# Second slice finished in sorted order, with rows that carry x1, gate, probability and place, and the first slice's rows modulated by GpSimd

## What is computed

```
mod = (silu(c) @ wmod) -> sa, ca, ga, sb, cb, gb            # per sequence, 128 each; ga, gb clamped away from 0
h  = layernorm(x) * (1 + ca) + sa
q, k = silu(h Wq), silu(h Wk);  k normalised;  v = h Wv;  beta = 2 sigmoid(h Wbet);  a = sigmoid(h Wf)
for t: Sd = a_t S;  S = Sd + beta_t k_t (v_t - k_t Sd);  o_t = q_t S
x1 = x + ga * ((rmsnorm(o) * norm_w) @ Wo)
h  = layernorm(x1) * (1 + cb) + sb
route = softmax(h @ router_w + router_b);  e = argmax, p = max
out = x1 + gb * p * (silu(h W1a[e]) * (h W1b[e])) @ W2[e]
```

## Time and profile before

| | us |
|---|---|
| median of 3 runs | 469.03 (467.74 to 471.08) |
| profiled execution, its time | 469.78 |
| profiled execution, its span | 468.0 |
| busy: DVE / PE / ACT / POOL | 377.9 / 368.5 / 281.0 / 276.6 |
| recurrence ends (last products on DVE) | 303.2 |
| last `sum_outputs` ends | 307.0 |
| last expert matmul ends | 453.2 |

### The profile page before, as it was taken

The page is one execution under the profiler, slowest core; times in us unless marked ns, Lnnn a source line. Parts: engine busy times, 40 slices in busy tenths (PEclk is TensorE's granted clock), DMA queues, the critical chain, the costliest instruction groups (busy, mean ns, idle before and its releaser), DMA issues.

```text
span 468.0 us, 8624 instructions
## 1 busy us (share of the span) xinstructions
PE 368.5 (79%) x2495; PEld 317.9 (68%) x2495; DVE 377.9 (81%) x1143; ACT 281.0 (60%) x634; POOL 276.6 (59%) x339
## 2 busy tenths in 40 slices
PE   3867853938779996993867866879989999999970
PEld 2322410728567766993967866879888999999970
DVE  4859999999998999999997999976828445569634
ACT  3589766956357466586646626374774657566520
POOL 1036234999999949757678198704185556653340
PEclk9989987878879999898698796999999999999995
DMA  8184888992000002923200004117411114155006
GB/s 229 39 118 94 109 114 119 137 127 3 0 1 1 1 1 90 373 78 66 71 0 1 1 7 117 60 41 162 150 30 41 41 41 115 46 164 139 28 34 179
DMA packets 49502, 37.13 MB, mean 79 GB/s; under 512 B 11088, under 2 KB 45200, under 8 KB 49328
## 3 DMA queue, kind: packets, MB, share of 16 engines
q1 hardware_dynamic: 46064, 30.39, 32.9%
q0 software_dynamic: 3392, 6.18, 4.3%
HBM read 17.36 MB, written 10.29 MB: 59 GB/s over the span
## 4 chain that ended last, share of the span: by engine, by line
PE 32%; DVE 30%; POOL 13%; issue 11%; ACT 7%; DMA 6%; SPq 1%; ACTq 0%; POOLq 0%; DVEq 0%
PE bank L900 9%; PE bank L636 6%; DVE U L1797 6%; DVE S L1810 5%; DVE p L1791 5%; DVE p L1804 4%; PE bank L917 4%; PE bank L693 3%; POOL sorted_h L1085 3%; POOL big L1019 2%; DMA sorted_h<-X,pos 2%; POOL prod_o L308 2%; ACT ph L1197 2%; PE bank L638 1%; PE bank L697 1%
## 5 line engine op out<-in xcount | busy, mean ns | idle before, releaser
L693 PE MATMUL bank<-prod_o,ID 128*128 128x128 f32 x512 | 75.5, 308 | 30.3 <-POOL prod_o L315 18.4
L900 PE MATMUL bank<-Q,p 128*128 128x128 f32 x736 | 94.2, 275 | 1.2 <-ACT p L1507 1.2
L693 PEld LDWEIGHTS bank<-prod_o,ID 128*128 128x128 f32 x512 | 70.5, 219 | 33.1 <-POOL prod_o L315 21.7
L900 PEld LDWEIGHTS bank<-Q,p 128*128 128x128 f32 x736 | 89.0, 192 | 1.5 <-ACT p L1507 1.4
L1312 ACT ACTIVATE p<-S,GAM 128x64 f32<-128x64 f32 x126 | 48.4, 410 | 66.9 <-DVE S L1810 66.2
L308 POOL TENSOR_TENSOR prod_o<-Q,ST 128x1024 f32<-128x1024 f32 x28 | 60.0, 2143 | 29.4 <-PE bank L697 29.2
L1143 POOL DMA_INDIRECT placed_y<-Q,place x46 | 44.4, 965 | 49.4 <-DVE place L2003 17.9
L1507 ACT ACTIVATE p<-big 128x1024 f32 x46 | 48.5, 1057 | 40.9 <-PE bank L900 38.9
L1810 DVE TENSOR_REDUCE S<-p 128x64 f32<-128x320 f32 x126 | 55.8, 475 | 0.0
L1797 DVE TENSOR_REDUCE U<-p 128x32 f32<-128x288 f32 x128 | 52.2, 442 | 0.0
L1791 DVE TENSOR_TENSOR p<-S,bank 128x256 f32<-128x256 f32 x128 | 48.7, 410 | 0.7 <-ACT bank L1307 0.7
(11 more groups left out here) (265 smaller groups left out, 746.1 us busy)
## 6 DMA issues: line engine op xcount, KB each, us to landing
big<-in_L_ffn_w_dram SPq DMA_DIRECT2D x1, 4096.0 KB, 14.1
big<-big SPq DMA_DIRECT2D x16, 192.0 KB, 4.5
Q<-sorted_h SPq DMA_DIRECT2D x46, 64.5 KB, 2.2
sorted_h<-ZERO SPq DMA_DIRECT2D x2, 1472.0 KB, 17.8
X<-in_L_attn_x_dram SPq DMA_DIRECT2D x8, 256.0 KB, 4.6
big<-big SPq DMA_DIRECT2D x16, 128.0 KB, 5.4
K<-placed_y SPq DMA_DIRECT2D x8, 256.0 KB, 3.2
out_dram<-X SPq DMA_DIRECT2D x8, 256.0 KB, 2.4
```

Of the source, the lines that this page charges most:

```text
L693: pe.matmul(ps, ID[:, :], prod_o[:, k % 2, i, :], start=(i == 0), stop=False, skip_group_check=True)
L900: m = pe.matmul(bank[(1, 6)[g % 2] + k][:, c * P:(c + 1) * P], W1E[g % 2][:, f:f + P], XST[:, g % 3, :], start=True, stop=True)
```

## The change

Second slice. The rows scattered to `sorted_h[1]` are 386 floats wide instead of 129: the modulated row, x1, the gate row gb, the place and the probability. x1 is written by `attend` on DVE straight into the wide rows (X1), the gates are loaded into them (GB, now two transfers, issued when the variances of slice 1 are there), and the probability too, so `exponentials(1)` moves on ACT from g = 22 to g = 10 and `probability(1)` on DVE to just ahead of `sort(1)`. `ys` for g >= 23 is two DVE instructions: result * probability * gate, then + x1; POOL scatters this straight to `out`, with a bounds check that drops the padding rows. `load_y`, `finish` and `store_out` of slice 1 are gone, and so are the sixteen L2091. The padding on SP grows from four to seven transfers. A ring slot of slice 1 is free only when `ys` has used the row.

First slice. PE turns the normalised tiles, ACT copies them unmodulated (`copy_turned_first`, four of 128x512), the router's weights carry the scale and ones times the shift (`modulate_router`, moved on POOL from behind the loop to g = 7). `shift2`, `shift_rows`, `turn_back` and `rows` are gone. POOL modulates the rows behind `make_products(11, 1)`, eight instructions, with scales and shifts that SP spreads earlier. `logits(0)` and `sort(0)` come one chunk earlier on DVE. On POOL the first burst of six scatters lies behind `make_products(12, 1)`, the second of five between (13, 0) and (13, 1), the third of five behind (13, 1); before, six lay between (13, 0) and (13, 1) and ten behind.

```diff
-    AT_SHIFT = (AT_ROWS + 2, AT_ROWS + 4)
-    SHIFT_AT = {AT_ROWS + 3: (1,), AT_ROWS + 4: (3,)}
-    H2_AT = {AT_ROWS + 3: (0,), AT_ROWS + 4: (1,), AT_ROWS + 5: (2,), AT_ROWS + 6: (3,)}
-    AT_ROUTE, AT_SORT, AT_EXP = AT_ROWS + 5, AT_ROWS + 7, AT_ROWS + 10
+    TURNED_AT = {AT_ROWS + 3: (0, 1), AT_ROWS + 4: (2, 3)}
+    AT_ROUTE, AT_SORT, AT_EXP = AT_ROWS + 4, AT_ROWS + 6, AT_ROWS + 10
...
+    D1, D3 = D + 1, 3 * D + 2
+    ROW_W, AT_PLACE = (D1, D3), (D, 3 * D)
+    sorted_h = [nc.dram_tensor(f"sorted_h{s}", (NFE, ROW_W[s]), F32, kind="Internal").ap() for s in range(NTIME)]
+    placed_y = nc.dram_tensor("placed_y", (B * N + NFE, D), F32, kind="Internal").ap()
...
+    out_rows = out.rearrange("b n d -> (b n) d")
...
-                sp.dma_start(rows[:, :, 0:D], ZERO[:, :].unsqueeze(1).broadcast_to([P, NF, D])).then_inc(sem("padded"), 16)
+                for part_of_row in range(0, AT_PLACE[s], D):
+                    sp.dma_start(rows[:, :, part_of_row:part_of_row + D], ZERO[:, :].unsqueeze(1).broadcast_to([P, NF, D]))\
+                        .then_inc(sem("padded"), 16)
...
+            sp.wait_ge(sem("att_ps", 0), 4)
+            for h in range(NHALF):
+                spread_rows(h, 1, SCALES[0][h])
...
-                if g >= XR:
+                if j == 0 and s == 1:
+                    sp.wait_ge(sem("place_ready"), NF)
+                if g - XR >= NF:
+                    sp.wait_ge(sem("ys_ready"), g - XR + 1)
+                elif g >= XR:
...
-                    sp.wait_ge(sem("att_ps", 1), 4)
-                    sp.dma_start(GB[:, :, :].rearrange("p b d -> p (b d)"),
-                                 gate_h.rearrange("(a x) -> a x", a=1).broadcast_to([P, B * D])).then_inc(sem("gb_in"), 16)
+                    sp.wait_ge(sem("root_in"), ASKED)
+                    for h in range(NHALF):
+                        sp.dma_start(GB[h], gate_h.rearrange("(b d) -> b d", d=D)[h * HB:(h + 1) * HB, :].unsqueeze(0)
+                                     .broadcast_to([P, HB, D])).then_inc(sem("gb_in"), 16)
...
-            for q in range(4):
-                load_y(sp, 1, q)
-            for q in range(4):
-                store_out(sp, 1, q)
-            sp.wait_ge(sem("stored"), 16 * 8)
+            sp.wait_ge(sem("stored"), 16 * 4)
+            results_out(sp, NTIME * NF)
...
                 if g == G_TURN:
-                    for q in range(3):
+                    for q in (0, 1):
                         turn_rows2(q)
-                    weigh_experts(0)
-                    turn_back(0)
-                    turn_rows2(3)
-                    weigh_experts(1)
-                    turn_back(1)
+                    for q in (0, 1):
+                        weigh_experts(q)
+                        turn_rows2(2 + q)
                     for q in (2, 3):
                         weigh_experts(q)
-                    for q in (2, 3):
-                        turn_back(q)
...
                     if g == G_SORT:
-                        if h == 0:
-                            place_rows(0)
-                        sort_rows(0, h)
-                if g == G_SORT:
-                    sort_rows(0, 2)
+                        sort_rows(0, 1 + h)
+                if g == G_SORT - 1:
+                    sort_rows(0, 0)
+                if g == G_TURN + 1:
+                    place_rows(0)
+                    for q in range(4):
+                        modulate_rows(q)
...
+                if g < NF:
+                    out_dma = pool.indirect_dma_start(placed_y, at, YS[:, g % YR, :], None)
+                else:
+                    out_dma = pool.indirect_dma_start(out_rows, at, YS[:, g % YR, :], None, bounds_check=B * N - 1, oob_is_err=False)
...
+            def copy_turned_first(q):
+
+                act.wait_ge(sem("xn2t_ps"), q + 1)
+                if q >= 2:
+                    act.wait_ge(sem("lg_ps"), q - 1)
+                act.activation(H2T[:, q % 2, :], TURN_BANKS[0][q][:, :], ACT.Copy).then_inc(sem("turned_in"), 1)
...
-                if g == NF - 1:
+                if g == F_ROUTE:
                     exponentials(1)
...
+                if s == 0:
+                    link(dve.reciprocal(maxp[:, :], posf[:, :]))
+                else:
+                    for h in range(NHALF):
+                        dve.reciprocal(H2[1][h][:, :, D3 - 1], posf[:, h * HB:(h + 1) * HB]).then_inc(sem("row_parts"), 1)
...
-                yield from after_chunk(AT_SHIFT[0] - 1)
-                yield from slots(NHALF * 2)
-                shift2(0)
-                yield from after_chunk(AT_SHIFT[1] - 1)
-                yield
-                shift2(2)
                 yield from after_chunk(AT_ROUTE - 1)
...
-                dve.tensor_copy(YS[:, g % YR, :], result(g)).then_inc(sem("ys_ready"), 1)
...
+                if g < NF:
+                    dve.tensor_copy(YS[:, g % YR, :], result(g)).then_inc(sem("ys_ready"), 1)
+                else:
+                    row = sorted_rows(g)
+                    yield from settle(dve.scalar_tensor_tensor(out=YS[:, g % YR, :], in0=result(g), scalar=row[:, D3 - 1:D3],
+                                                               in1=row[:, 2 * D:3 * D], op0=ALU.mult, op1=ALU.mult))
+                    dve.tensor_tensor(YS[:, g % YR, :], YS[:, g % YR, :], row[:, D:2 * D], ALU.add).then_inc(sem("ys_ready"), 1)
...
                 if g == F_ROUTE + 1:
+                    probability(1)
                     now(sort(1))
                     now(sorted_places(1))
```

More of the change, by code:

```diff
@@ L180, in adaln_block @@
         place = sb("place", [P, 2 * NF], U32)
-        maxp = [sb(f"maxp{h}", [P, NT]) for h in range(NHALF)]
+        maxp = sb("maxp", [P, NT])
         tex = [sb(f"tex{h}", [P, NF], I32) for h in range(NHALF)]
@@ L1125, in _ @@
                     decay_queries(Q_AT.index(g), 1)
+                if g == G_SCALE - 1:
+                    modulate_router()
                 if g == G_SCALE:
@@ L1440, in _ @@
                     scale_rows(n - AT_ROWS - 1)
-                for q in SHIFT_AT.get(n, ()):
-                    shift_rows(q)
-                for q in H2_AT.get(n, ()):
-                    rows(q)
+                for q in TURNED_AT.get(n, ()):
+                    copy_turned_first(q)
                 if n % GC == GC - 2 and n // GC + 1 < NG:
@@ L1599, in stats, with stats_x1 @@
                 link(last)
+            def stats_x1(tiles):
+                for t in tiles:
+                    last = dve.bn_stats(st[:, t, :], X1[t // HB][:, t % HB, :])
+                link(last)
             def variances():
@@ L1604, in variances, with scale_x1 @@
                 yield from ask_root(last)
+            def scale_x1(tiles):
+                dve.wait_ge(sem("xn2t_ps"), 4)
+                for t in tiles:
+                    dve.tensor_scalar(XNB[:, t, :], X1[t // HB][:, t % HB, :], mv[:, t, 0:1], yy[:, t:t + 1], ALU.subtract, ALU.mult)\
+                        .then_inc(sem("xn2_ready", 1), 1)
             def scale(h, tile, XN, ready, tiles):
-                if ready == "xn2_ready" and h == 1:
-                    dve.wait_ge(sem("xn2t_ps"), 4)
                 for t in tiles:
@@ L1901, in sorted_places @@
                 dve.wait_ge(sem("pos_ready"), s + 1)
-            def shift2(k):
-                dve.wait_ge(sem("xn2t_ps"), k + 1)
-                if k >= 2:
-                    dve.wait_ge(sem("shifted"), 4 * k)
-                    dve.wait_ge(sem("h2_ps"), k - 1)
-                for i in range(4):
-                    b = 4 * (k % 4) + i
-                    dve.tensor_scalar(H2T[:, k % 2, i * P:(i + 1) * P], TURN_BANKS[k // 4][k % 4][:, i * P:(i + 1) * P],
-                                      MOD[:, 3, b:b + 1], MOD[:, 2, b:b + 1], ALU.mult, ALU.add).then_inc(sem("shifted"), 1)
             chunk = [-1]
@@ L2047, in _ @@
                         dve.wait_ge(sem("ys_ready"), YACT)
-                    ys(g - 3)
+                    out_of = ys(g - 3)
+                    next(out_of, None)
                 if g + 2 < G and g + 2 not in (NF, NF + 1):
                     xst(g + 2)
+                now(out_of)
                 if g == 0:
@@ L2067, in _ @@
                     shifts()
-                    scale(1, second_tile, XNB, "xn2_ready", range(NT // 2))
+                    scale_x1(range(NT // 2))
                 if g == F_ROUTE:
@@ L2086, in _ @@
                 if NF + YIN - 2 <= g < NF + YIN + 2:
[L2087 to L2093 removed]
+                    finish(g - NF - YIN + 2)
 _INS = ["L0_attn_x", "L0_attn_Wq", "L0_attn_Wk", "L0_attn_Wv", "L0_attn_Wo", "L0_attn_Wbet", "L0_attn_Wf", "L0_attn_norm_w",
```

199 lines of the change are left out of this document (86 added, 113 removed).

## The result

| | before | after |
|---|---|---|
| median, us | 469.5 (467.65 to 471.08, 16 runs) | 473.44 (471.38 to 475.89, 16 runs) |
| profiled execution: span, time | 468.0, 469.78 | 470.6, 472.35 |

The ratio is 1.0085, with a 95% interval of 1.0068 to 1.0102: 0.85% slower, +3.9 us (3.2 to 4.8). The forecast was 464.5 with a range of 460.5 to 468.5, so the time lies outside it and on the other side of the time before.

What follows compares the result with a forecast made beforehand. The prediction took DVE as the bound up to 303 us, PE to 453, then a serial tail of 15 us. Terms -10.7 + 3.0 + 0.7 + 2.3 + 0.2 = -4.5 us took the median from 469.03 to 464.5, range 460.5 to 468.5.

Steps and rivals of the forecast that it cites:

- tail: Behind the last matmul: slice 1's loads, finish and stores go, new end 457.3 instead of 468.0; -10.7 us (-9.8 to -11.0).
- recurrence's end: First slice: POOL's products (13, 1) come 4.8 us late behind eleven scatters, not six; +3.0 us (+1.9 to +4.0).
- probability, route: Slice 1's route: three small DVE instructions of `probability(1)` ahead of `sort(1)`, PE waiting behind the sort; +0.7 us.
- boundary: Slice 1's scatters and first loads: wider rows land later in four bursts, PE stands; +2.3 us (0.5 to 3.5).
- finish, second instruction of `ys`: Slice 1's tiles: at g = 33 to 36 DVE falls about 1 us behind, of which PE feels 0.2.
- longer issues of wide scatters: Rival: issue grows with the bytes, sixteen in series before PE's next tile; doubled, 15.4 us, time 480; chance 0.07.
- four route instructions: First slice's route on DVE: both inputs in SBUF, blocked beside POOL's modulation; 0.75 each, 3.0 us (1.0 to 4.0).
- At nothing: Parts of the change that the prediction described but costed at zero or nearly so.
- three more padding transfers: On SP: some 15 us, with nothing else to issue between 99.8 and 182.8; costed at nothing.
- the exponential beside tile 10: On ACT: two table loads of 1.28 at g = 10, costed at nothing; 2.9 us without cover.
- the waits of the loads for `ys`: Loads for g >= 30 wait for `ys(g - 7)`, 5.6 us ahead of their turn, and take about 3; costed at nothing.
- rival of the starved ring: Slice 1's tiles: loads waiting for `ys` come 0.4 us late at each of sixteen tiles, 6.4; time 471; chance 0.06.

## Why the prediction was wrong, step by step

The sum again, with what the stretches show:

| term | predicted | measured | from |
|---|---|---|---|
| tail | -10.7 | -2.9 | last matmul's end to the span's, 468.0 - 453.2 = 14.8 before, 470.6 - 458.7 = 11.9 after |
| recurrence's end | +3.0 | +1.8 | (11, 1) to tile 2, means of the table |
| probability, route | +0.7 | +0.4 | tile 2 to 22: 69.1 and 69.5, means |
| boundary | +2.3 | +3.2 | tile 22 to 27: 14.8 and 18.05, means |
| finish, second instruction of `ys` | +0.2 | +0.7 | tile 27 to 45: 0.36 more, means of the same seven; 45 to the last matmul: 0.34 |
| sum | -4.5 | +3.2 | times: +3.9 (3.2 to 4.8) |

"Means" are of the five traces with narrow rows and the seven with wide rows in four bursts.

**The tail is the step that failed.** I followed the chain from the last scatter to its landing, 456.82, and put the new end there at 457.3. The chain was right for what it named; it did not name what was hidden beside it. The row of GpSimd's DRAIN, 453.5 to 464.2, stood in the trace of before, in the engine's sequencer and not among the busy instructions, and the prediction does not speak of it. With it the term is bounded by 467.8 - 464.2 = 3.6 us: the sum becomes +2.6 (+3.2 with the measured sizes), slower as measured. The term missed by 10.7 - 2.9 = 7.8 us. Leaving the DRAIN out brings back 7.3 of them by the stretch (11.9 to 4.6; 7.8 by the times, with an interval of over 1 us either way). The other 0.5 is the prediction's own: 457.3 is 4.1 us behind the last matmul, and without a DRAIN the end comes 4.6 behind it. (The term's smaller bound was added wrong, too: 0.7 + 0.9 off 11.2 is -9.6, not -9.8. It changes nothing here.) None of the rivals in the prediction was this one; on the slower side it had longer issues of wide scatters, and of those nothing happened: 0.96 us each, 1.26 apart, as in the earlier trace rows.

**The recurrence** went as described, nearly step for step. The rows of DVE and PE after:

```profile
255.63 0.29 DVE L1851 TENSOR_TENSOR RT<-bank,RB 128x128 f32<-128x128 f32 x1 [4.75 <-PE bank L810]
...
257.01 1.36 DVE L1860 TENSOR_TENSOR RT<-RT,lmx 128x128 f32<-128x128 f32 x1
...
258.69 0.94 DVE L1861 TENSOR_TENSOR RT<-RT,rev 128x128 f32<-128x128 f32 x1
```

```profile
292.43 3.73 PE L712 MATMUL bank<-prod_o,ID 128*128 128x128 f32 x16 [5.32 <-POOL prod_o L326]
```

DVE stood 4.75 us for its logits (I had 3.4; my own 256.1 - 252.9 gives 3.2). POOL modulated from 254.4 to 264.5 in eight instructions of 1.18 to 1.32. Its products (13, 1) started at 289.09, 2.7 us later than in the earlier trace rows in an execution that was 2.1 ahead at (11, 1), so 4.8 late as forecast, and PE waited 5.32 us for them. In this pair of executions the whole term is +2.8 (60.8 and 58.0 us), as forecast; on the means of the table it is +1.8. Two sizes were off, one in each direction: DVE stood longer, while the four route instructions with both inputs in SBUF took 1.36, 0.94, 0.43 and 0.39 us beside GpSimd, 2.0 more in all and not 3.0. Two of the four stood long, two hardly at all. By the Trainium skill ("SBUF — State Buffer", § SBUF: two separate sides) the one that comes second is held until the other ends; the rows agree, with its price being what happens to be left. And the owner of the term was booked wrong: it stands under the rows on GpSimd, with the bursts only as a part of it. The rows alone give 1.9 to 2.2 us back (stretch and times), and the burst's place takes 3.75. The old order with the new rows would have been the better change (469.58, and 466.52 without the second slice's part), and the working had the numbers for it: "eleven scatters now lie ahead of it and not six".

**The boundary** was under-sized, mostly by the clock. The landing waits grew by less than I took: 2.03, 2.05, 2.08 and 2.93 us for the four bursts against 2.04, 1.68, 1.66 and 2.53 before, 1.2 together and not 1.6. The rest was larger: PE stood 1.58, 0.21 and 0.44 us where it had stood 0.20, and behind the stand it ran at the lower clock level: 1.52 and 2.79 in the two rows of L901 above, 1.06 and 1.95 at the upper one, 1.3 us more. I had charged no clock to a wait of PE, though the same effect is in the earlier trace rows and I used it there. The two traces in which the clock stayed up have +2.5 on the mean, near the forecast of 2.3; the five with the lower level have +3.5. What decides between them is open. The estimate by the page "DMA: Bandwidth & Descriptors" of the Trainium skill (§ Anatomy of one DMA — SWDGE (gpsimd) path), 1.5, was further off for the same reason; its 0.3 for each burst is what the four bursts show on the mean.

**At nothing** stood three more padding transfers, the exponential beside tile 10 and the waits of the loads for `ys`. For the first two nothing in the stretches speaks against it. The third is not quite nothing. It is the prediction's rival of the starved ring, once in a program and not sixteen times: in five of the thirteen traces with wide rows PE stands 0.4 to 0.9 us for the load of tile 42, as in the row with 0.92 above. The margin was also smaller than forecast, 4.7 us from issue to turn and not 5.6. In the profiled execution of the changed kernel PE doesn't stand there. The second instruction of `ys` lasts 0.28 us, and the finish and the last results together cost 0.7 in all.

## What to carry to other kernels

Before booking a tail as gained, list what ends under it on every engine, the sequencers too, and take the latest of those as the new end; a closing row on an engine that was off the chain is the first suspect. An edit that moves two things on one engine's queue (rows and bursts) gets two terms, since one may gain what the other loses. And a new wait of PE gets a range: without slower matmuls behind it, and with them, from a row at either level.

## What the runs showed of the hardware

GpSimd's DRAIN took 8.7 us after 106 of its DMAs, 8.3 after 101, 8.2 after 100 and 1.4 after five, all of them landed or not. Where another engine waits for each DMA's semaphore, as SP does here, the program can end without it: 7.8 us earlier where nothing covered it, no earlier where the last loads and stores did. The issue of a scatter did not grow with its rows: 0.96 us for 516 and for 1,544 bytes a row, 0.98 with a bounds check, whose results landed in 2.7 us at the median against 2.4. GpSimd's wait for the last landing of a set of scatters varied between 1.9 and 4.3 us from one trace to the next, with no cause found. And where the wide rows in four bursts made PE stand 2.1 to 2.8 us in all, the granted clock fell to its lower level for 3.4 us in five of seven traces, and stayed up in two.
